# A transformer layer on one core: GpSimd's tiny multiplications that carried waits become semaphore increments

## What is computed

```python
x = x + 0.5 * ffn(layernorm(x))
x = x + attention(layernorm(x))
x = x + 0.5 * ffn(layernorm(x))

def ffn(h):                     # E = 8 experts, K = 2 per token, hidden size 352; shared part 176
    top_v, top_i = top_k(h @ gate_w, 2)
    combine = zeros(T, 8).at[arange(T)[:, None], top_i].add(softmax(top_v))
    d = einsum('tei,eih->teh', silu(h @ Wg[e]) * (h @ Wu[e]), Wd)
    return einsum('te,teh->th', combine, d) + silu(h @ Sg) * (h @ Su) @ Sd

def attention(h):               # linear attention, 16 heads of size 8, along the 32 sequences
    q, k, v = split(h @ W_attn + b_attn);  q, k = elu(q) + 1, elu(k) + 1
    # running sums over the first axis of k (x) v and of k; y = q.kv / (q.ksum + 1e-6)
    return y @ W_proj + b_proj
```

## Time and profile before

| | us |
|---|---|
| median of three executions | 1369.38 |
| fastest, slowest of them | 1367.43, 1383.91 |
| span of the profiled execution, first to last instruction | 1240.9 |
| median less that span | 128.5 |
| TensorE (PE) busy | 989.7 |
| VectorE (DVE) busy | 896.8 |
| GpSimd (POOL) busy | 843.8 |
| ScalarE (ACT) busy | 669.6 |

### The profile page before, as it was taken

One profiled execution on the slowest core, in us unless ns is written; L12 is line 12 of the kernel. 1 busy time (PEld: TensorE's weight loads), 2 busy tenths in 40 slices (PEclk: granted clock), 3 DMA queues, 4 the chain that ended last, 5 costly groups with the idle time before them and its releaser, 6 DMA issues. The chain is left out here.

```text
span 1240.9 us, 31979 instructions
## 1 busy us (share of the span) xinstructions
PE 989.7 (80%) x8996; PEld 742.7 (60%) x8997; DVE 896.8 (72%) x2369; ACT 669.6 (54%) x1466; POOL 843.8 (68%) x872
## 2 busy tenths in 40 slices
PE   2657665999999927788888888888864999999940
PEld 1434344899989924455555555555543888899930
DVE  6778784676676745788888888888854666666748
ACT  4556642555555523466665656666331555555545
POOL 4677773777777845467787787778642677777750
PEclk9898996999999968999999999999966999999985
DMA  9411122222222221001111111100003222222229
GB/s 279 108 51 47 52 76 66 78 79 76 78 77 78 68 59 33 17 33 37 34 34 51 34 38 41 41 17 18 23 27 87 74 74 77 78 75 78 73 95 332
DMA packets 68607, 86.62 MB, mean 70 GB/s; under 512 B 13004, under 2 KB 56209, under 8 KB 68558
## 3 DMA queue, kind: packets, MB, share of 16 engines
q1 hardware_dynamic: 51278, 52.15, 14.5%
q0 software_dynamic: 17280, 33.87, 8.3%
HBM read 44.74 MB, written 43.04 MB: 71 GB/s over the span
## 5 line engine op out<-in xcount | busy, mean ns | idle before, releaser
L496 POOL DMA_INDIRECT expert_results<-ey,eidx x284 | 293.3, 1033 | 70.9 <-issue 69.6
L485 POOL DMA_INDIRECT routed_rows<-row,idx x256 | 255.2, 997 | 73.6 <-issue 70.2
L1142 DVE SCALAR_TENSOR_TENSOR ehT<-eh,ehT 128x768 f16<-128x768 f32 x142 | 136.1, 958 | 150.1 <-ACT ehT L688 150.1
L683 ACT ACTIVATE esil<-PSUM 128x768 f32<-128x768 f32 x142 | 115.1, 810 | 230.2 <-PE PSUM L826 224.6
L824 PE MATMUL PSUM<-eT,WGU 128*128 128x256 f16 x852 | 234.3, 275 | 1.4
L825 PE MATMUL PSUM<-eT,WGU 128*128 128x256 f16 x852 | 233.9, 275 | 0.0
L826 PE MATMUL PSUM<-eT,WGU 128*128 128x256 f16 x852 | 233.8, 274 | 0.0
L510 POOL TENSOR_TENSOR space<-qk,val 128x1152 f32<-128x1152 f32 x64 | 138.2, 2171 | 69.5 <-DVE shift L1192 48.7
L824 PE MATMUL PSUM<-WD,ehT 128*128 x852 | 161.0, 220 | 8.3 <-DVE ehT L1142 5.0
L825 PE MATMUL PSUM<-WD,ehT 128*128 x852 | 159.3, 220 | 0.0
L826 PE MATMUL PSUM<-WD,ehT 128*128 x852 | 158.8, 219 | 0.0
(11 more groups left out here) (197 smaller groups left out, 2300.0 us busy)
## 6 DMA issues: line engine op xcount, KB each, us to landing
xe<-routed_rows SPq DMA_DIRECT2D x142, 130.0 KB, 2.1
space<-expert_results SPq DMA_DIRECT2D x32, 512.0 KB, 3.9
expert_results<-ey,eidx POOLq DMA_INDIRECT x284
X<-in_L_attn_x_dram SPq DMA_DIRECT2D x16, 256.0 KB, 4.6
routed_rows<-row,idx POOLq DMA_INDIRECT x256, 2.3
out_dram<-X SPq DMA_DIRECT2D x16, 256.0 KB, 4.3
routed_rows<-pad_rows SPq DMA_DIRECT2D x24, 130.0 KB
space<-in_L_ffn_Wg_dram SPq DMA_DIRECT2D x1, 1408.0 KB, 9.1
```

Source lines behind the costliest of these rows:

```text
L485: pool.indirect_dma_start(routed, bass.IndirectOffsetOnAxis(ap=idx[u][:, k, j:j + 1], axis=0), row[u][:, j, :], None).then_inc(s_scattered ...
L496: pool.indirect_dma_start(result, bass.IndirectOffsetOnAxis(ap=eidx[u][:, h:h + 1], axis=0), ey[u][:, h, :], None, bounds_check=K * T - 1, ...
L683: act.activation(esil[u][:, :], PSUM[:, 1536 * u:1536 * u + 768], ACT.Silu, scale=2.0 ** -(SX + SWT)).then_inc(s_block_silu, 1)
L1142: return dve.scalar_tensor_tensor(out=dst, in0=src, scalar=float(2 ** scale), in1=high, op0=ALU.mult, op1=ALU.subtract)
```

## The change

The two multiplications and their tiles go. In their places stands a semaphore increment on GpSimd (`s_scatter_begun`, `s_results_begun`), which nobody waits for. The waits of DVE for `s_ticket` and of ACT for `s_carrier` are deleted, so that these engines rest on `s_scattered` and `s_results`, which the DMAs themselves increment when they have landed, and for which there were waits before. The drain L491 goes too.

```diff
-        carrier = sb("carrier", [P, 2])
-        ticket = sb("ticket", [P, ROWS_AHEAD])
...
-        s_carrier = sem("s_carrier")
-        s_ticket = sem("s_ticket")
+        s_scatter_begun, s_results_begun = sem("s_scatter_begun"), sem("s_results_begun")
...
             def scatter(n, u):
                 pool.wait_ge(s_placed_rows, n + 1)
                 pool.wait_ge(s_row_words, n + 1)
-                pool.tensor_tensor(ticket[:, u:u + 1], ones32[:, 0:1], ones32[:, 0:1], ALU.mult).then_inc(s_ticket, 1)
+                pool.sem_inc(s_scatter_begun, 1)
                 for k in range(K):
                     for j in range(NJ):
...
                 if isinstance(n, int) and n in (NBLK - 1, 2 * NBLK - 1):
-                    pool.drain().then_inc(s_carrier, 1)
                     return
                 pool.wait_ge(s_block_results, n + 1)
-                pool.tensor_tensor(carrier[:, u:u + 1], ones32[:, 0:1], ones32[:, 0:1], ALU.mult).then_inc(s_carrier, 1)
+                pool.sem_inc(s_results_begun, 1)
...
                 wait(act, s_results[u], res_value(n, u))
-                wait(act, s_carrier, n - 1)
...
                 dve.drain()
-                wait(dve, s_ticket, n - 1)
                 dve.tensor_reduce(idx[u][:, :, :], pk[:, :, :, :], AX.X, ALU.max).then_inc(s_placed_rows, 1)
```

## The result

The changed kernel takes 1425.36 us (median of 4, 1418.86 to 1429.04) where the kernel before takes 1373.35 (median of 4): ratio 1.038, 95% interval 1.0329 to 1.0431. It is slower by 3.8%, or 52 us; 1366.2 was predicted, with a range of 1356 to 1377.

A forecast was written before the change was run, and what follows sets the result against it. PE was taken to bound the expert passes and POOL the first token pass. Gains of 1.1 + 0.2 + 0.7 + 1.2 = 3.2 us off 1369.4 gave 1366.2 us, range 1356 to 1377.

The forecast's parts named there:

- with 128.5 us around it unchanged: Whole kernel: the profiled span of 1240.9 us plus 128.5 us outside it makes the timed 1369.4.
- Carriers: Expert passes: 140 of 142 multiplications lie hidden beside PE's work, worth nothing; the pass ends gain 0.7 us together.
- Tickets, streams: Streams: 15 of 16 ticket multiplications are worth nothing, the last gives 0 to 0.3 us; 0.2 taken.
- A block would gain 0.44 if the cover were gone: Expert passes: without PE's longer work per block, removing the multiplication would save 0.59 + 0.15 - 0.30 us.
- I take 0.45: End of each expert pass: last `ey` to its DMA falls from 0.81 to 0.45 us, gaining 0.36 per pass.
- Tickets, first token pass: First token pass: shorter boundaries between scatters from group 11 on gain 1.1 us.
- POOL's lag late in the passes: Late in each expert pass: DMAs may slip out from under `ehT`, gaining 0.6 us each, 1.2 together.
- The phase end: End of each expert pass: POOL's later drain delays the release, hidden behind load waits by 0.5 and 0.4 us.
- The increment costs what the multiplication cost: POOL's DMAs: the increment runs in order and start-up remains, so all gains vanish: 1369.4 us, chance 0.14.
- A late first DMA: Expert passes: DMA start-up after the wait grows, PE waits 0.2 us in each of 142 blocks: 1398, chance 0.04.
- More DMAs meet DVE: Last five groups of the first token pass: shifted scatters are held up under DVE more often: 1371.2, chance 0.15.
- The chain is right: Expert passes: POOL paces the blocks, so 142 x 0.44 = 62 us go: 1307, chance 0.03.

The follow-up runs named there:

- the tickets alone: Kernel before with only the 32 ticket multiplications made increments and DVE's wait removed: 1244.25 us, ratio 1.0031; again, 1391.65 against 1377.23, ratio 1.0115.
- the light kernels: Kernel before and changed kernel, each with one matmul in place of three in both products of an expert-pass block: 1163.03 and 1163.59 us.
- the waits replaced: Changed kernel with long-fulfilled waits where ACT's and DVE's waits on POOL had been: 1430.01 us, ratio 1.0423 to the kernel before.
- the carriers alone: Kernel before with only the 142 carrier multiplications made increments, ACT's wait and POOL's drain removed: 1239.05 us, ratio 0.9985; again, 1401.14, ratio 1.0209.
- the waits kept: Kernel before with both multiplications made increments, all waits and drains kept: 1241.39 us, ratio 0.9997; again, 1428.50 against 1374.15, ratio 1.0394.

## Why the prediction was wrong

*The base.* The step that failed is "with 128.5 us around it unchanged". I read a span of 1240.9 beside a time of 1369.38, wrote the difference down as lying outside, and took every cover from that page. Nothing lies outside but 1.8 us; the timed runs have their 130 us more inside: 37 in the first token pass, 40 and 45 in the expert passes, 7 in the streams, none in the last stage. With the page's own time (1241) as base, the sum would have read 1238; measured there are 1242.6 to 1244.4, 0.1 to 0.2% above the kernel before, with intervals that reach 1. With the timed runs as base, PE was not the bound that never rests. The wrong base alone does not make 52 us: what failed with it are the terms that had been put at nothing, or nearly, under cover of that page, the next two.

*Carriers "beside PE's work: cost and gain nothing".* True in the 1241 condition (254.3 against 255.0 us for the first pass). In the condition that was timed it is false: with 15 us of rest in 160, PE covers less, and ACT's late `esil`s, which stop PE too, became nearly twice as many. The expert passes have 17 + 12 us of the 54 by which the two traces differ.

*Tickets, streams, "0 to 0.3 us; I take 0.2".* In the 1370 condition the tickets alone lose 24 us there (522.7 against 499.0), and the whole change 17. In the 1241 condition the term lies below what the traces scatter.

*The price of a multiplication.* "A block would gain 0.44 if the cover were gone" and "I take 0.45" for the last transfer of a pass were both mis-sized. The transfer starts 0.04 us later without it (0.87 us for the last one of the first pass too), and with POOL never at rest a multiplication costs 0.09. The multiplication's 0.59 was read as its own work, and the increment, taken at nothing everywhere, costs 0.08 behind a wait.

*Tickets, first token pass.* Right in kind: the boundary is 0.30 and an increment behind a transfer costs nothing. 1.1 us was predicted, 0.5 to 0.7 gained, in the 1241 condition.

*POOL's lag late in the passes.* The coin fell the other way. Every second transfer is still held up under `ehT` from 406.83 on, and ACT still waits 2.08 us for a landing before 443.88, where it waited 1.96. So nothing of the 1.2 us came. The rule taken from the row of 1.72 us held: in the traces of the kernel before and of the changed one in the 1241 condition, 24 and 19 transfers of results start under `ehT`; they take up to 1.74 us, and all end 0.84 to 0.86 us behind it.

*The phase end.* The rows that answer to the earlier trace rows, in the changed kernel in the 1241 condition:

```profile
451.37 0.81 SPq L393 DMA_DIRECT2D space<-expert_results  x2
453.92 0.35 DVE L1526 TENSOR_SCALAR row<-row 128x4 f32<-128x4 f32 x2 [11.13 <-POOLq L252]
455.41 0.88 DVE L1333 SCALAR_TENSOR_TENSOR X<-space,PR,X 128x128 f32<-128x128 f32 x3 [1.14 <-DMA space<-expert_results]
```

As predicted, the release comes later behind SyncE's load, 2.55 us and not 1.60, and is hidden: DVE's first large instruction still waits for its load.

*The rivals.* "The increment costs what the multiplication cost" describes the 1241 condition: gains near zero, and mostly for the reason given there, start-up; behind a wait the increment even costs a little more. "A late first DMA" had the right sign and half the size (1398) at a chance of 0.04. But its mechanism, a longer start-up that PE waits for, is not what happened: the transfer starts 0.04 us later in the 1241 condition and 0.06 in the other (0.87 against 0.81), where more than 0.8 were wanted. That its direction came true was luck. "More DMAs meet DVE" is there in small: the scatters from group 11 on take 0.4 us more, where 3.8 were feared. (Its bound was misread: four meetings of 0.76 us are 3.0, less than the gain of 3.2.) "The chain is right" is answered by the light kernels: with POOL never at rest, 0 us are gained in 142 blocks, not 62. No rival had a kernel that is slow in another way than the page shows.

*What stays open.* What the 3 us are, and why an increment in place of a multiplication nearly doubles their number. In the seven traces of the 1370 condition, without the first and last four blocks of each pass, 208 of 882 `esil`s are late. In 167 of these, two of POOL's transfers start between 1.9 us before and 0.2 us behind the moment at which the product is ready; of the 674 that are in time only 11 have this. That is a coincidence in time and not yet a cause: in the light kernels of the 1241 condition 214 of 252 blocks have it too, and only 5 of them are over 1 us late. The condition could be met and not made. That the exchange of POOL's multiplications for increments brings the loss is shown; by which way is not. The 9 us more in the first token pass (241.0 and 241.8 in the changed kernel, 241.2 with the waits replaced, but 232.0 with the tickets alone, 233.1 with the carriers alone and 234.5 with the waits kept) are not explained either. In this pass, then, the waits may have a part, though the total shows none.

The Trainium skill, "Runtime: NRT & Kernel Launch", section "Instruction fetch mechanics", says that a taken branch to a page of instructions outside the current window stops an engine until it is fetched. No run here shows what is fetched. It could make PE and ACT stand at once, but by itself it says nothing about POOL's increments.

## What to carry to other kernels

Hold the span of the profiled execution against the timed runs before anything else. If they differ by more than a few microseconds, the profile is not of what was timed, and its covers and slacks don't hold there. The price of an instruction in front of an indirect transfer is what the transfer's start moves, not the instruction's length: here a multiplication cost nothing behind a wait and 0.09 us between two transfers. An increment in its place was the other way round, 0.08 us behind a wait and nothing between two transfers. And compare two kernels side by side, on more than one chip and at more than one time: the same change cost 0.1 to 0.2%, hardly told from nothing, in three comparisons, and 3.7 and 3.8% in two others.

## What the runs showed of the hardware

- One program on one core has two levels of time, 1241 and 1372 us, 10% apart, at the same granted clock in the middle of the expert passes (1.00), and at 0.88 and 0.77 in the first token pass. In all eight comparisons the executions side by side shared the level; two chips showed both levels at different times.
- In the slower one ACT takes up a finished product 2.8 to 2.9 us late (median of each trace) in 19 to 38 of 142 blocks, and in most of them PE stands one to three times for half a microsecond in the same stretch, while POOL's transfers keep their 0.97 to 1.00 us. In the faster one neither kernel has such a block.
- An indirect transfer of POOL starts 0.83 us after ACT's `ey` with a multiplication of 0.59 us in between, and 0.87 us with a semaphore increment in its place, 1.11 with four increments. Between two transfers without a wait four increments leave the gap at 0.31 us.
- An indirect transfer of POOL that starts under DVE's `ehT` (two inputs, 0.96 us) ends 0.84 to 0.86 us behind the end of that instruction, in 24 of 24 cases in the kernel before and 19 of 19 in the changed one; alone it takes 0.97 to 1.00.
- Copies of 1.44 MB on ACT's queue (34.60 MB in all) make PE wait for SyncE's loads of rows up to 10.4 us at a time.
